# One core, Swin block then Fourier mix: the loop's tensor products in eight runs of one tile shape, joined log and root, normalisation in PSUM, eight buffers in the last stage

## The chip, the cores and the metric

One core of one Trainium2 chip runs the whole program in one launch. The time is device microseconds of that core, the median of several executions. TensorE (PE in the rows; PEld is its weight loading), VectorE (DVE), ScalarE (ACT) and GpSimd (POOL) each work through their own instructions in program order and wait for each other by semaphores; SyncE (SP) issues nearly all DMAs. A time difference of about 2% is what a comparison here calls a difference.

## The reference, cut to what matters

```python
def _L0_conv_ref(x, ...):                       # x: (8, 256, 256, 64) float32
    a = _shifted_window_attention(x, qkv_w, ...)  # windows of 4x4 tokens, 4 heads of 16
    x = x + _layernorm(a, norm1_g, norm1_b)
    h = gelu(x @ fc1_w.T + fc1_b) @ fc2_w.T + fc2_b          # 64 -> 256 -> 64
    x = x + _layernorm(h, norm2_g, norm2_b)
    return x
# inside the attention, for each window and head:
    qn = q / max(norm(q), 1e-12); kn = k / max(norm(k), 1e-12)
    attn = softmax(qn @ kn.T * scale + bias)     # 16 x 16
    out = (attn @ v) @ proj_w.T + proj_b
def _L1_conv_ref(x, w_real, w_imag):
    trend = _moving_average(x, 25)               # along axis 1, 256 long
    xf = rfft(x - trend, axis=1)[:, :128]
    ys = einsum('bmnc,cmk->bknc', xf, w_real + 1j * w_imag)
    return trend + irfft(ys padded with zeros, n=256, axis=1)
```

## The kernel before, in words

Everything is float32. The program has three stages. First a short one makes for each of the 64 channels the 256x256 matrix that stands for the whole second layer (moving average, transform, mixing, inverse) and stores it in `mix`. Then the **loop** does the first layer. Last, the **final stage** multiplies, for each of 8 images and 64 channels, the channel's matrix (`amat`) with the channel's plane (`xch`), 8 records of 256 columns on TensorE (L581), copies the product from a PSUM bank into `orow`, ScalarE the even channels (`put`, L718) and VectorE the odd ones (L912), and after each image lets ScalarE's queue store 16.8 MB (four DMAs of 4096 KB). It has `NB` = 4 buffers of `amat` and `xch` and uses 4 PSUM banks; both puts of an image wait until the image before is stored.

The loop runs over 512 groups of 512 tokens as a pipeline written out by hand: in step s every engine does a fixed list of small functions, each for the group of its stage, `i0` = s, `i1` = s-1, up to `i7` = s-7. The order of the calls at the end of each engine's `step` is the order on the engine; no scheduler moves anything. `need(engine, semaphore, group)` waits, `.then_inc(semaphore)` signals, and `there(g)` leaves a function out where its group doesn't exist. `over_groups` runs 16 steps written out, then a loop, then 7 steps that empty the pipeline.

TensorE, with the tile shape (rows x columns of the array) of each function: `turn_x` (L450, 128x128) transposes the tokens; `project_qkv` (L462, 64x128) two halves; `scores` (L479, 32x32) two parts of 64 products, each recorded as two; `weighted` (L501, 32x32) two halves; `project` (L513, 128x64); `variances` (L526 and L530, 64x64) of both layernorms; `first_layer` (L542, 64x128) and `second_layer` (L554, 128x64), two halves each. ScalarE: `keep_x` L622, `square` L629, `log_norm` L634, `root_norm` L641, `exponent` L647, `keep_o` L653, `square1` L660, `square2` L677, log and root of the two layernorms L665, L671, L682, L688, `gelu` L694 twice, and two loads of a function table (L696, L706), because Gelu and Ln/Exp lie in different tables. VectorE: `qkv_out` L805 (twice), `sum_squares` L813, `clamp` L819, `turn_k` L825, `turn_q` L831, `bias` L836, `maximum` L844, `sum_prob` L850, `invert` L857, `turn_prob` L863, `normed1` L869, `add1` L877, `normed2` L883, `gain2` L889. GpSimd: `add_o1` L944, `expand_v` L953 (two instructions), `scale_norm` L961, `norm_k` L967, `norm_q` L976, `shift` L985, `divide` L991, `add_o2` L997, `add2` L1008. SyncE loads x, 8 DMAs for a group, swaps halves of `sq1` and stores a stripe of y every four groups.

The norms of q and k go through this sequence: `square`, `sum_squares`, `clamp`, `log_norm`, `root_norm`, then `scale_norm`, `norm_k` and `norm_q` on GpSimd, then the transposes `turn_k` and `turn_q` on VectorE, then the scores:

```python
def clamp(g):                                   # VectorE, 128x64, SBUF to SBUF
    need(dve, summed, g)
    ts(ssc[ring(g, 2)], ss, 1e-24, None, ALU.max).then_inc(clamped, 1)
def log_norm(g):                                # ScalarE
    need(act, clamped, g)
```

## Time and profile before

| | before |
|---|---|
| median of three executions | 8558.72 us (lowest 8556.22) |
| profiled execution: its time | 8548.61 us |
| profiled execution: span, first to last instruction | 8546.5 us |
| TensorE busy | 8028.8 us, 94% of the span |
| VectorE, ScalarE, GpSimd busy | 5981.4, 6209.3, 5385.1 us |
| mean granted TensorE clock | 0.971 |
| chain that ended last: TensorE's share | 72% |

The loop's first transpose (L450) starts at 272.4 us and its last at 7211.5 us; the puts of the final stage start at 7313 us. Busy TensorE is an engine with something in its pipe, not one at its peak. In a timeline row the columns are the start, the time from the first start to the last end, the engine, the line, the operation, the tensors, and the count; idle time before it stands in brackets with what ended it.

### The profile page before, as it was taken

The page shows a single profiled execution, that of the slowest core. Times are in us where ns is not written, and L with a number is a line of the kernel's source. Part 1 is how long each engine was busy: PE and PEld are TensorE (multiplying, and loading weights), DVE is VectorE, ACT ScalarE, POOL GpSimd, SP SyncE. Part 2 cuts the span into 40 slices and gives each one's busy share as a digit, 9 for nine tenths or more (in the row PEclk, how much of TensorE's full clock was granted, in tenths as well). Part 3 has the DMA queues.
Part 4 walks back from the last instruction along what each step waited for, and adds up shares of the span by engine and source line. Part 5 has one row for each costly group of instructions (what it writes and reads, how often), then busy time and mean ns, then how long its engine had stood idle before and what let it go on. Part 6 is the DMA issues. An engine that isn't in the chain of part 4 may idle for free.

```text
span 8546.5 us, 659317 instructions
## 1 busy us (share of the span) xinstructions
PE 8028.8 (94%) x293684; PEld 5312.2 (62%) x293684; DVE 5981.4 (70%) x8029; ACT 6209.3 (73%) x8530; POOL 5385.1 (63%) x5127
## 2 busy tenths in 40 slices
PE   8899999999999999999999999999999999787786
PEld 5556666666666666666666666666666665566565
DVE  1468888888888888888888888888888887222221
ACT  1478888888888888888888888888888888222221
POOL 0367777777777777777777777777777777000000
PEclk9799999999999999999999999999999999898898
DMA  3122222222222222222222222222222222799999
GB/s 99 53 50 58 58 58 59 59 59 59 59 58 59 59 59 59 58 59 58 59 59 59 58 57 57 58 59 59 59 58 59 59 58 55 269 317 329 330 318 334
DMA packets 1187111, 834.30 MB, mean 98 GB/s; under 512 B 633233, under 2 KB 1043217, under 8 KB 1182867
## 3 DMA queue, kind: packets, MB, share of 16 engines
q1 hardware_dynamic: 1182404, 698.61, 31.9%
q10 hardware_dynamic: 4608, 134.22, 3.7%
q8 instruction: 80, 1.31, 0.1%
q14 instruction: 19, 0.16, 0.0%
HBM read 412.97 MB, written 285.21 MB: 82 GB/s over the span
## 4 chain that ended last, share of the span: by engine, by line
PE 72%; SPq 14%; DMA 7%; issue 4%; ACT 2%; ACTq 0%; DVE 0%; POOL 0%; POOLq 0%; DVEq 0%
PE ps L501 12%; PE ps L479 11%; PE ps L581 10%; SPq L335 10%; PE ps L554 8%; PE ps L542 8%; PE ps L462 8%; PE ps L526 5%; PE ps L513 5%; DMA out<-arena 3%; DMA arena<-in_x 3%; PE ps L450 3%; SPq L346 2%; SPq L341 2%; PE ps L424 1%
## 5 line engine op out<-in xcount | busy, mean ns | idle before, releaser
L953 POOL TENSOR_TENSOR arena<-arena 128x512 f32<-128x512 f32 x1024 | 1043.5, 1040 | 894.2 <-PE ps L501 894.2
L479 PEld LDWEIGHTS ps<-arena 32*32 32x32 f32 x131072 | 1236.4, 106 | 508.4 <-issue 502.0
L501 PEld LDWEIGHTS ps<-arena 32*32 32x32 f32 x131072 | 1289.3, 103 | 292.8 <-issue 259.1
L501 PE MATMUL ps<-arena 32*32 32x16 f32 x131072 | 1424.4, 186 | 21.1 <-issue 19.5
L479 PE MATMUL ps<-arena 32*32 32x16 f32 x131072 | 1345.1, 180 | 23.3 <-issue 16.2
L805 DVE TENSOR_TENSOR arena<-ps,arena 128x768 f32<-128x768 f32 x1024 | 980.7, 958 | 370.1 <-PE ps L462 358.0
L581 PE MATMUL ps<-xch,amat 128*128 128x256 f32 x4096 | 924.3, 389 | 285.4 <-ACT arena L718 169.5
L462 PEld LDWEIGHTS ps<-arena 64*128 64x128 f32 x8192 | 649.1, 188 | 837.4 <-issue 825.5
L985 POOL TENSOR_TENSOR arena<-arena 128x512 f32<-128x512 f32 x512 | 713.5, 1394 | 696.2 <-DVE arena L844 696.2
L694 ACT ACTIVATE arena<-ps,arena 128x1024 f32<-128x1024 f32 x1024 | 1137.4, 1111 | 7.0 <-PE ps L542 0.4
L581 PEld LDWEIGHTS ps<-xch,amat 128*128 128x128 f32 x4096 | 786.6, 195 | 423.5 <-ACT arena L718 174.7
L542 PE MATMUL ps<-arena 64*128 64x512 f32 x4096 | 1032.4, 621 | 2.8 <-ACT arena L682 2.3
L554 PE MATMUL ps<-arena 128*64 128x512 f32 x4096 | 999.9, 607 | 4.0 <-ACT arena L694 3.1
L462 PE MATMUL ps<-arena 64*128 64x192 f32 x8192 | 954.3, 352 | 5.7 <-DVE arena L805 3.2
L718 ACT ACTIVATE arena<-ps 128x512 f32 x256 | 271.0, 1066 | 935.4 <-PE ps L581 608.6
L912 DVE COPY arena<-ps 128x512 f32 x256 | 267.9, 1052 | 940.2 <-PE ps L581 625.4
L877 DVE SCALAR_TENSOR_TENSOR arena<-arena 128x512 f32<-128x512 f32 x512 | 829.9, 1621 | 23.6 <-PE ps L542 23.4
L991 POOL TENSOR_TENSOR arena<-arena 128x512 f32<-128x512 f32 x512 | 841.5, 1644 | 0.1
L665 ACT ACTIVATE arena<-ps,arena 128x512 f32<-128x512 f32 x512 | 352.0, 688 | 508.1 <-PE ps L530 505.5
L836 DVE TENSOR_TENSOR arena<-ps,arena 128x512 f32<-128x512 f32 x512 | 354.2, 692 | 515.9 <-PE ps L479 512.9
L944 POOL TENSOR_TENSOR arena<-arena 128x512 f32<-128x512 f32 x512 | 535.4, 1046 | 276.0 <-ACT arena L622 271.9
L813 DVE TENSOR_REDUCE arena<-arena 128x64 f32<-128x1024 f32 x512 | 624.9, 1220 | 106.4 <-ACT arena L629 84.0
(89 smaller groups left out, 14288.3 us busy)
## 6 DMA issues: line engine op xcount, KB each, us to landing
arena<-in_x SPq DMA_DIRECT2D x4096, 32.0 KB
arena<-arena SPq DMA_DIRECT2D x1024, 128.0 KB
y<-ystripe SPq DMA_DIRECT2D x256, 512.0 KB
amat<-mix SPq DMA_DIRECT2D x512, 256.0 KB, 3.4
xch<-y SPq DMA_DIRECT2D x512, 256.0 KB, 4.0
out<-arena ACTq DMA_DIRECT2D x32, 4096.0 KB, 27.1
mix<-amat SPq DMA_DIRECT2D x64, 256.0 KB, 2.0
wri<-in_w_real SPq DMA_DIRECT2D x64, 64.0 KB, 1.8
```

Of the source, the lines that this page charges most:

```text
L335: sp.dma_start(xin[:, p, a * C:a * C + C], src[:, p * 8:p * 8 + 8, :]).then_inc(x_in, 16)
L462: ins = mm(M[:, a, pl * 256:pl * 256 + 3 * C], xT[a * C:a * C + C, 2 * pp + pl, :], wqkv[a * C:a * C + C, :], start=True, stop=True, tile_ ...
L479: ins = mm(S(sl)[r, c0 + e:c0 + 32:2], qT[r, sl, q, e:64:2], kT[r, sl, q, e:32:2], start=True, stop=True, tile_position=(32 * cg, 32 * cg))
L501: ins = mm(PV[32 * h:32 * h + 32, b, c0:c0 + N], vexp[r, sl, h, :, :], pT[r, sl, h // 2, h % 2, :], start=True, stop=True, tile_position=( ...
L542: ins = mm(M[:, a, :], w1[a * C:a * C + C, kk * P:(kk + 1) * P], x1T[a * C:a * C + C, :], start=True, stop=True, tile_position=(a * C, 0))
L554: ins = mm(H2[a * C:a * C + C, :], w2[:, kk, :], hT[kk][:, a, :], start=(kk == 0), stop=(kk == 1), tile_position=(0, a * C))
L581: ins = mm(ps[:, j, k * T:(k + 1) * T], amat[j][:, r * T + k * P:r * T + (k + 1) * P], xch[j][:, r * T:(r + 1) * T], start=(r == 0), stop= ...
L694: f(hT[kk], M, ACT.Gelu, bias=b1[:, kk:kk + 1]).then_inc(done, 1)
L805: tt(qkv[ring(g, 4)][:, :, 4 * pp:4 * pp + 4, :].rearrange("p w s n -> p s w n"), M.rearrange("p a (s n) -> p (a s) n", s=2)[:, :, 0:3 * C ...
L877: stt(x1T, dn1, g1, xTo[ring(g, 4)], ALU.mult, ALU.add).then_inc(x1_sb, 1)
L953: tt(vexp.rearrange("p s h e d -> p (s h) e d")[:, :, e, :], qkv[ring(g, 4)][:, 2].rearrange("p s (h d) -> p (s h) d", h=HEADS), par[:, e: ...
L991: tt(pr, pr, rs.rearrange("p (n e) -> p n e", e=2).unsqueeze(2).to_broadcast([P, N, N, 2]), ALU.mult).then_inc(probs, 1)
```

## The change

TensorE's calls are put in an order in which neighbours have the same tile shape: both parts of `scores` become one run, `project` stands before `second_layer`, both halves of `project_qkv` are neighbours and get different PSUM banks (MA and MB), and `variances` comes before `first_layer`. There are 8 runs in place of 11 in a step. So that this is possible, `variances` writes to banks 4 and 5 (where scores and weighted values lie), no longer to banks 2 and 3. The logs of the two layernorms become one 128x1024 instruction, their roots another. `normed1` writes its result back to PSUM (`D1`), and `add1` reads it there; `project` therefore waits for `add1`. All lists of calls on ScalarE, VectorE and GpSimd are written in another order, with other stages for some. The final stage has `NB` = 8.

```diff
-        NB = 4
+        NB = 8
...
-        VV = MB
+        VV = ps[:, 4:6, :]
...
+        def need_norms(eng, s, g, h):
+            if there(g) or there(h):
+                eng.wait_ge(s, h.base + (h.off + 3))
...
                 def turn_x(g):
-                        after(pe, (gelu0, i6), (l1_sb, i5, i7), (xT_sb, before(g)))
+                        after(pe, (gelu1, i6), (qkvB_sb, before(g)))
                 def scores(g):
+                        if there(i5) or there(i7):
+                            need_norms(pe, l12_sb, i5, i7)
                 def project(g):
-                        need(pe, dn1_sb, before(g))
+                        need(pe, x1_sb, before(g))
                 def variances(g, h):
-                        after(pe, (xT_sb, i0), (gelu0, i6), (l1_sb, before(g), before(h)))
+                            need(pe, oT_sb, i3)
                 def first_layer(g, kk, M, done):
-                            after(pe, (l1_sb, i4, i6), (xT_sb, i0), (gelu0, before(g)))
+                            after(pe, (qkvA_sb, i0), (gelu0, before(g)))
-                            after(pe, (qkvB_sb, i0), (qkvA_sb, i0), (gelu1, before(g)))
+                            after(pe, (qkvB_sb, i0), (gelu1, before(g)))
-                scores(i2, 0)
+                scores(i2)
                 project(i4)
-                turn_x(i0)
-                scores(i2, 1)
                 second_layer(i6, 0, fc2a_ps)
                 second_layer(i6, 1, fc2b_ps)
+                weighted(i3, 0, pvA_ps)
+                turn_x(i0)
+                weighted(i3, 1, pvB_ps)
                 project_qkv(i0, 0, MA, qkvA_ps)
-                weighted(i3, 0, pvA_ps)
+                project_qkv(i0, 1, MB, qkvB_ps)
                 variances(i4, i6)
-                project_qkv(i0, 1, MA, qkvB_ps)
-                weighted(i3, 1, pvB_ps)
-                first_layer(i5, 0, MB, fc1a_ps)
-                first_layer(i5, 1, MA, fc1b_ps)
+                first_layer(i5, 0, MA, fc1a_ps)
+                first_layer(i5, 1, MB, fc1b_ps)
...
+                def log_norms(g, h):
+                    if there(g) or there(h):
+                        need_norms(act, var_ps, g, h)
+                        k = slice(0 if there(g) else 1, 2 if there(h) else 1)
+                        f(l12[:, k, :], VV[:, k, :], ACT.Ln, bias=eps).then_inc(l12_sb, 1)
+                def root_norms(g, h):
+                    if there(g) or there(h):
+                        need_norms(act, l12_sb, g, h)
+                        need(act, dn1_sb, before(g))
+                        need(act, dn2_sb, before(h))
+                        k = slice(0 if there(g) else 1, 2 if there(h) else 1)
+                        f(r12[:, k, :], l12[:, k, :], ACT.Exp, scale=-0.5).then_inc(r12_sb, 1)
...
-                act.preload_act_table_set(EXP_SET)
-                log_norm(i2)
-                square2(i7)
-                root_norm(i2)
-                exponent(i3)
-                log1(i5)
-                log2(i7)
-                root1(i5)
-                root2(i7)
-                keep_o(i4)
-                act.preload_act_table_set(GELU_SET)
-                gelu(i6, 0, MB, fc1a_ps, fc2a_ps, gelu0)
+                gelu(i6, 0, MA, fc1a_ps, fc2a_ps, gelu0)
+                gelu(i6, 1, MB, fc1b_ps, fc2b_ps, gelu1)
                 square(i1)
                 square1(i4)
-                gelu(i6, 1, MA, fc1b_ps, fc2b_ps, gelu1)
+                act.preload_act_table_set(EXP_SET)
+                log_norm(i1)
+                root_norm(i1)
                 keep_x(i0)
+                square2(i6)
+                keep_o(i3)
+                exponent(i2)
+                log_norms(i4, i6)
+                root_norms(i4, i6)
+                act.preload_act_table_set(GELU_SET)
...
-                        stt(dn1, D1, be1, r1, ALU.add, ALU.mult).then_inc(dn1_sb, 1)
+                        stt(D1, D1, be1, r12[:, 0, :], ALU.add, ALU.mult).then_inc(dn1_sb, 1)
-                        stt(x1T, dn1, g1, xTo[ring(g, 4)], ALU.mult, ALU.add).then_inc(x1_sb, 1)
+                        stt(x1T, D1, g1, xTo[ring(g, 4)], ALU.mult, ALU.add).then_inc(x1_sb, 1)
-                        stt(dn2, H2, be2, r2, ALU.add, ALU.mult).then_inc(dn2_sb, 1)
+                        stt(dn2, H2, be2, r12[:, 1, :], ALU.add, ALU.mult).then_inc(dn2_sb, 1)
```

The new lists of VectorE and GpSimd are shown below as they stand on the engines.

TensorE, one turn of the loop before (`scores`, `project`, `turn_x`, `scores`, `second_layer`, `project_qkv`, `weighted`, `variances`, `project_qkv`, `weighted`, `first_layer`):

```order
L479 MATMUL ps<-arena 32x16 x64
L228 REGISTER_ALU
L513 MATMUL ps<-arena 64x4x64 x4
L228 ISA
L228 REGISTER_ALU
L450 MATMUL ps<-arena 128x128 x4
L479 MATMUL ps<-arena 32x16 x64
L228 REGISTER_ALU
L554 MATMUL ps<-arena 64x512 x4
L228 REGISTER_ALU
L462 MATMUL ps<-arena 128x192 x4
L228 REGISTER_ALU
```

and the same turn of the changed kernel, to its end (L477 is now `scores`, L557 `second_layer`, L448 `turn_x`, L458 `project_qkv`, L529 and L533 `variances`, L545 `first_layer`):

```order
L477 MATMUL ps<-arena 32x16 x128
L228 REGISTER_ALU
L513 MATMUL ps<-arena 64x4x64 x4
L228 REGISTER_ALU x2
L557 MATMUL ps<-arena 64x512 x4
L228 REGISTER_ALU
L501 MATMUL ps<-arena 32x16 x64
L228 ISA
L448 MATMUL ps<-arena 128x128 x4
L501 MATMUL ps<-arena 32x16 x64
L228 REGISTER_ALU
L458 MATMUL ps<-arena 128x192 x8
```

The scores stand in one row of 128, and the two halves of `project_qkv` in one of 8; `variances` and `first_layer` follow them.

VectorE before, from `turn_q` to `gain2`:

```order
L831 STREAM_TRANSPOSE arena<-arena 128x1024
L869 SCALAR_TENSOR_TENSOR arena<-ps,arena 128x512
L883 SCALAR_TENSOR_TENSOR arena<-ps,arena 128x512
L857 RECIPROCAL arena<-arena 128x32
L877 SCALAR_TENSOR_TENSOR arena<-arena 128x512
L813 TENSOR_REDUCE arena<-arena 128x64
L836 TENSOR_TENSOR arena<-ps,arena 128x512
L863 STREAM_TRANSPOSE arena<-arena 128x512
L819 TENSOR_SCALAR arena<-arena 128x64
L844 TENSOR_REDUCE arena<-arena 128x32
L889 TENSOR_SCALAR arena<-arena 128x512
```

and of the changed kernel from `gain2` (L881), `sum_squares` (L805), `clamp` (L811), `turn_k` (L817), `qkv_out` twice (L797), `turn_q` (L823), `sum_prob` (L842), `invert` (L849) to `normed1` (L861) and `add1` (L869); `normed2`, `bias`, `turn_prob` and `maximum` (L836) follow and close the turn:

```order
L881 TENSOR_SCALAR arena<-arena 128x512
L805 TENSOR_REDUCE arena<-arena 128x64
L811 TENSOR_SCALAR arena<-arena 128x64
L817 STREAM_TRANSPOSE arena<-arena 128x512
L228 REGISTER_ALU
L797 TENSOR_TENSOR arena<-ps,arena 128x4x3x64 x2
L823 STREAM_TRANSPOSE arena<-arena 128x1024
L842 TENSOR_REDUCE arena<-arena 128x32
L849 RECIPROCAL arena<-arena 128x32
L861 SCALAR_TENSOR_TENSOR ps<-ps,arena 128x512
L869 SCALAR_TENSOR_TENSOR arena<-ps,arena 128x512
```

The clamp, which stood ahead of `maximum`, now stands two places behind `gain2`.

GpSimd of the changed kernel, one turn: `divide`, `add_o2`, `add_o1`, `shift`, `add2` (L1000), `scale_norm` (L953), `norm_k`, `norm_q`, `expand_v`:

```order
L983 TENSOR_TENSOR arena<-arena 128x512
L989 TENSOR_TENSOR arena<-arena 128x512
L228 REGISTER_ALU
L936 TENSOR_TENSOR arena<-arena 128x512
L977 TENSOR_TENSOR arena<-arena 128x512
L1000 TENSOR_TENSOR ystripe<-arena 128x8x16x4
L953 TENSOR_TENSOR arena<-arena 128x32
L959 TENSOR_TENSOR arena<-arena 128x512
L968 TENSOR_TENSOR arena<-arena 128x16x2x16
L945 TENSOR_TENSOR arena<-arena 128x32x16 x2
```

Before, `add2` stood behind `expand_v`; now it stands between `shift` and `scale_norm`.

## Rows read from the trace of the kernel before

**Rows 1.** Windows of L450 alone: us, engine busy (records), granted clock, DMA, GB/s

```profile
560.00:7200.00 6640.00, 323.30 (x1972) 207.51 (x1972) 1.00 0.26 58
272.00:560.00 288.00, 15.46 (x72) 9.93 (x72) 0.78 0.18 40
```

**Rows 2.** Waits of PE from 560 to 7200 us: total, times, longest

```profile
PE ps L450 <- DMA arena<-in_x: 47.0, 123, 0.6
```

**Rows 3.** Timeline of PE over one step

```profile
4013.03 1.99 PE L542 MATMUL ps<-arena 64*128 64x512 f32 x8
4014.95 1.26 PE L479 MATMUL ps<-arena 32*32 32x16 f32 x128
4016.15 1.08 PE L513 MATMUL ps<-arena 128*64 128x256 f32 x8
4017.16 0.66 PE L450 MATMUL ps<-arena 128*128 128x128 f32 x4
...
4018.94 1.94 PE L554 MATMUL ps<-arena 128*64 128x512 f32 x8
4020.81 0.92 PE L462 MATMUL ps<-arena 64*128 64x192 f32 x8
4021.66 1.42 PE L501 MATMUL ps<-arena 32*32 32x16 f32 x128
...
4026.37 1.99 PE L542 MATMUL ps<-arena 64*128 64x512 f32 x8
```

**Rows 4.** Timeline of DVE in one step

```profile
4012.84 1.23 DVE L831 STREAM_TRANSPOSE arena<-arena 128x1024 f32<-128x1024 f32 x1
...
4013.99 0.71 DVE L869 SCALAR_TENSOR_TENSOR arena<-ps,arena 128x512 f32<-128x512 f32 x1
...
4014.62 0.73 DVE L883 SCALAR_TENSOR_TENSOR arena<-ps,arena 128x512 f32<-128x512 f32 x1
...
4015.54 1.56 DVE L877 SCALAR_TENSOR_TENSOR arena<-arena 128x512 f32<-128x512 f32 x1
```

**Rows 5.** Groups by line and form, all engines: count, busy us, mean ns, idle before

```profile
L479 PE MATMUL ps<-arena 32*32 32x16 f32 x131072 | 1345.1, 180 | 23.3 <-issue 16.2 <-DVE arena L831 4.9 <-ACT arena L653 1.8
...
L694 ACT ACTIVATE arena<-ps,arena 128x1024 f32<-128x1024 f32 x1024 | 1137.4, 1111 | 7.0 <-PE ps L542 0.4
...
L805 DVE TENSOR_TENSOR arena<-ps,arena 128x768 f32<-128x768 f32 x1024 | 980.7, 958 | 370.1 <-PE ps L462 358.0
...
L836 DVE TENSOR_TENSOR arena<-ps,arena 128x512 f32<-128x512 f32 x512 | 354.2, 692 | 515.9 <-PE ps L479 512.9 <-issue 3.0
...
L985 POOL TENSOR_TENSOR arena<-arena 128x512 f32<-128x512 f32 x512 | 713.5, 1394 | 696.2 <-DVE arena L844 696.2
```

**Rows 6.** Timeline of the first groups, 283 to 286 us

```profile
283.67 0.26 ACT L634 ACTIVATE arena<-arena 128x64 f32<-128x64 f32 x1
283.96 0.35 ACT L641 ACTIVATE arena<-arena 128x64 f32<-128x64 f32 x1
...
284.39 0.24 POOL L961 TENSOR_TENSOR arena<-arena 128x32 f32<-128x32 f32 x1 [9.03 <-ACT arena L641]
284.58 1.05 POOL L967 TENSOR_TENSOR arena<-arena 128x512 f32<-128x512 f32 x1
...
285.67 0.71 DVE L825 STREAM_TRANSPOSE arena<-arena 128x512 f32<-128x512 f32 x1 [0.60 <-POOL arena L967]
```

**Rows 7.** Timeline of the last groups, 7257 to 7260 us

```profile
7257.28 1.04 POOL L997 TENSOR_TENSOR arena<-arena 128x512 f32<-128x512 f32 x1 [0.63 <-DVE arena L877]
7257.76 0.85 DVE L889 TENSOR_SCALAR arena<-arena 128x512 f32<-128x512 f32 x1
...
7258.69 1.27 POOL L1008 TENSOR_TENSOR ystripe<-arena 128x512 f32<-128x512 f32 x1 [0.36 <-DVE arena L889]
```

**Rows 8.** Windows of the final stage: us, busy PE, PEld, DVE, ACT, POOL, clock, DMA, GB/s

```profile
7425.00:7470.00 45.00, 7.91 (x28) 5.81 (x26) 0.56 (x2) 0.49 (x1) 0.00 (x0) 0.62 1.00 419
7480.00:7580.00 100.00, 100.00 (x460) 85.79 (x459) 30.02 (x29) 29.86 (x29) 0.00 (x0) 1.00 0.94 300
```

More of the change, by code:

```diff
@@ L456, in project_qkv @@
                             need(pe, xT_sb, g)
-                            after(pe, (gelu1, i6), (qkvB_sb, i1), (qkvA_sb, before(g)))
-                        else:
-                            after(pe, (qkvA_sb, i0), (gelu1, i6), (qkvB_sb, before(g)))
+                            after(pe, (gelu0, i6), (qkvA_sb, before(g)))
                         for pl in range(2):
@@ L490, in weighted @@
                             need(pe, v1_sb, g)
-                            after(pe, (biased, i2), (oT_sb, before(g)))
+                            if there(i2):
+                                need(pe, biased, i2)
+                            else:
+                                need_norms(pe, l12_sb, i5, i7)
                         else:
@@ L726, in _ @@
                 with act.Fori(0, NCH // NB) as cq:
-                    for j in (0, 2):
+                    for j in range(0, NB, 2):
                         put(b, cq, j)
@@ L889, in gain2 @@
                         ts(yg, dn2, g2, None, ALU.mult).then_inc(yg_sb, 1)
-                sum_prob(i3)
-                turn_k(i2)
-                qkv_out(i1, 1, MA, qkvB_ps, qkvB_sb)
-                turn_q(i2)
                 normed1(i5)
+                add1(i5)
                 normed2(i7)
-                invert(i3)
-                add1(i5)
-                sum_squares(i1)
                 bias(i2)
                 turn_prob(i3)
-                clamp(i1)
                 maximum(i2)
                 gain2(i7)
+                sum_squares(i1)
+                clamp(i1)
+                turn_k(i1)
                 qkv_out(i0, 0, MA, qkvA_ps, qkvA_sb)
+                qkv_out(i0, 1, MB, qkvB_ps, qkvB_sb)
+                turn_q(i1)
+                sum_prob(i2)
+                invert(i2)
             over_groups(dve, step, 4)
@@ L920, in _ @@
                 with dve.Fori(0, NCH // NB) as cq:
-                    for j in (1, 3):
+                    for j in range(1, NB, 2):
                         put(b, cq, j)
@@ L1010, in add2 @@
                            ALU.add).then_inc(y_sb, 1)
-                divide(i2)
-                add_o1(i0)
-                add_o2(i4)
-                shift(i1)
-                scale_norm(i0)
-                norm_k(i0)
-                norm_q(i0)
-                expand_v(i1)
-                add2(i6)
+                divide(i3)
+                add_o2(i5)
+                add_o1(i1)
+                shift(i2)
+                add2(i7)
+                scale_norm(i1)
+                norm_k(i1)
+                norm_q(i1)
+                expand_v(i2)
             over_groups(pool, step, 8)
```

61 lines of the change are left out of this document (20 added, 41 removed).

## The prediction

> **What bounds the kernel now.** I read the windows first, because the loop is most of the span. The loop's steps follow each other at a steady 13.47 us: 1972 records of L450 in 6640 us are 493 steps of four, at a granted clock of 1.00 [rows 1]. The reader is to see next that TensorE hardly waits there: the answer on its waits has one line, 47.0 us for the DMA of x, 0.10 us a step [rows 2]. So the step is the sum of TensorE's runs. One step without such a wait, from one first layer to the next, takes 26.37 - 13.03 = 13.34 us [rows 3]. What the other engines do costs nothing as long as each of their loops is shorter than this. The timelines of VectorE and GpSimd [rows 4, 6, 7] are read for that: not how busy they are, but how long the shortest round through them is.
>
> **TensorE, step by step.** A run pays once for its change of tile shape, and this seam can be read off two runs of one shape. `project` streams 256 columns and takes 1.01 us to the start of the next run, `second_layer` streams 512 with as many records and takes 1.87 [rows 3]. So 256 columns are 0.86, and a seam is 1.01 - 0.86 = 0.15. For the 64x128 shape: 512 columns 1.92 us, 192 columns 0.85 [rows 3], so 320 columns are 1.07, 192 are 0.64, and the seam is 0.21. A part of the scores takes 1.20 to the next run; it is busy 1.26, of which the last record's own 0.18 is the tail [rows 3, 5], so its starts fill 1.08 and the seam is about 0.11. The change takes away one seam of each: 0.15 + 0.21 + 0.11 = 0.47 us. TensorE's own sum becomes 12.87. The bounds of this are nothing, if products that stand together still drain between them, and about 0.6, if the seams of the runs that got new neighbours shrink too.
>
> The Trainium skill says two things here. "TensorEngine Tiling (Array Packing)", section Key Properties, has a change of tiling mode drain the engine; "TensorE: Matmul & The Clock Gate", Part 2, lets the drain of one matmul overlap the fill of the next. By the second alone the seam would be nothing and TensorE's step would stay at 13.34; the rows' 0.15 to 0.21 side with the first.
>
> The wait for x goes: the loads of the next group are issued when the transposes are done, as before, but the transposes stand behind `weighted`, no longer behind `project`, so the queue, which first waits for `square1` and swaps halves, has some 2 us more before x is needed. That is 0.10 us a step. Moving the swaps' consumer to the step's end leaves them about as far ahead as now; no wait for a swap shows in the loop [rows 2], and I price that at zero.
>
> **New waits of TensorE.** The scores now wait for the joined log, because the variances lie in their banks, and `project` waits for `add1`, which had another wait before. Queued behind `project` is everything else. From the end of the variances: log and root as one 128x1024 instruction each, priced by the gelu's 1.11 [rows 5], then `normed1` 0.71 [rows 4], then `add1`, with some 0.04 for each release (285.63 to 285.67 is one [rows 6]). `add1` took 1.56 with two operands in SBUF, while the two instructions that read one operand from PSUM take 0.71 and 0.73 [rows 4]. It reads PSUM now, so I take 0.71, with 1.56 as the other end. The sum is 1.11 + 1.11 + 0.71 + 0.71 + 0.16 = 3.8 us. TensorE meanwhile has `first_layer` 1.92 and the scores, 1.20 + 1.08 = 2.28: 4.2 us, so nothing is lost, by 0.4 us. At 1.56 it would lack 0.45, and the step would be 13.3. That `normed1` writes PSUM has no row; I take its 0.71 unchanged, and up to 0.4 more would be hidden.
>
> **The round through VectorE, GpSimd and ScalarE.** This decides, and it is a chain of the new lists. In a full queue an instruction of VectorE follows the one before 0.08 us before its end (13.99 - 12.84 = 1.15 for 1.23 [rows 4]). From the start of `turn_k` to that of `maximum`, all in one list: `turn_k` 0.63, `qkv_out` twice 0.88, `turn_q` 1.15, `sum_prob` 0.73 (priced as a pass of 512 elements, 0.69, plus a release, since `invert` waits for it), `invert` and `normed2` together 15.54 - 14.62 = 0.92, `normed1` 0.75 with its release, `add1` 0.63, `bias` 0.61, `turn_prob` 0.63 [rows 4 to 6]. Together 7.81 us. Then `maximum`, 0.69 + 0.04, releases GpSimd's `shift`, 1.39 [rows 5], and behind it in GpSimd's queue is `add2`, 1.27 [rows 7], ahead of `scale_norm`. From there to `turn_k` of the next group, 285.67 - 284.39 = 1.28 [rows 6]. If nothing else enters, the round is 7.81 + 0.73 + 1.39 + 1.27 + 1.28 = 12.48: under TensorE's 12.87.
>
> But `clamp` enters. VectorE issues it after `maximum`, `gain2` and `sum_squares`: 0.61, 0.3 to 0.8 and about 1.23 (1024 elements, as `turn_q` [rows 4]), that is 2.1 to 2.6 us after the start of `maximum`. GpSimd's `add2` starts at 0.73 + 1.39 = 2.1 and ends at 3.4. So the clamp falls into `add2`, though perhaps by only 0.1 us at its front. What does a TENSOR_SCALAR from SBUF to SBUF do beside a GpSimd instruction? In the loop before none meets one, but among the last groups one does: `gain2`, issued at 7257.76, lasts 0.85, until 0.29 after GpSimd's L997 ends at 7258.32 [rows 7]. It waited for GpSimd. `clamp` is the same operation on fewer elements. I take it to wait too, and to end 0.10 after `add2` (between 0.05 and that 0.29). Then `log_norm` to `turn_k` follow, 0.04 and 285.67 - 283.67 = 2.00 [rows 6]. The round is 7.81 + 0.73 + 1.39 + 1.27 + 0.10 + 0.04 + 2.00 = 13.34 us, longer than TensorE's 12.87. ScalarE has its table loaded by then, and `keep_x` behind `root_norm` comes late as well, so that TensorE spends the difference, 0.47 us, before `project_qkv`.
>
> The Trainium skill's "SBUF — State Buffer", Who interferes with whom, says that a tensor_scalar in a two-port mode and a GpSimd instruction exclude each other for a whole instruction. By that rule the clamp waits and the step is the 13.34; row and rule agree, on another size of the same operation.
>
> **Final stage.** TensorE bounds it between stores: 8 records a channel, 460 in 100 us, 1.74 us a channel, while the DMAs move 300 GB/s; during a store they move 419 and TensorE stands [rows 8]. Eight buffers let TensorE do 4 channels more ahead of the wait, 4 x 1.74 = 7.0 us, seven times. But 4 channels more (4 x 0.52 MB = 2.1 MB) are then loaded beside the store, 2.1 MB / 419 GB/s = 5.0 us that the store takes longer. The net is 2 us, seven times: 14 us. The bounds are 0 and 49.
>
> **The sum.** Loop: 493 x (13.47 - 13.34) = 64 us. Final stage 14. The first and last groups stay. 8548.6 - 64 - 14 = 8471 for a profiled execution, and the median of the runs shown is 10 us above it: about **8480 us**. The round's terms are good for 0.2 us a step either way, 100 us, and its own range is 8385 to 8600.
>
> **Rivals.** First, the clamp doesn't wait for GpSimd, because it is small or slips in ahead of `add2`. Then TensorE's 12.87 bounds: 493 x 0.60 = 296 us, 8549 - 296 - 14 + 10 = 8249, and as low as 8190 with the larger seams. For it: no row shows a clamp waiting, and the margin at the front is 0.1 us. Against it: the row of `gain2`, and the two lists, which are timed by each other, so that the meeting recurs in every step. Second, the change doesn't do what it says: joined products drain as before, TensorE's step stays at 13.34 without the wait for x. That gives the forecast's own time by another way. Third, the slower side: the clock. Now it is 1.00 throughout the loop, but between 272 and 560 us, where the engines still wait for each other, it is granted at 0.78, and there 72 records are 18 steps in 288 us, 16.0 us each [rows 1]. The change brings 0.47 us of idle TensorE into each step, and puts both runs of `weighted` around the transposes. If that keeps the loop in the state of its first 288 us, it costs 493 x 2.53 = 1250 us, 9730 us. It decides from 0.35 us a step on, a seventh of that, which a mean clock of 0.97 in the loop would show. Against it: the wait at each step's x did not lower the clock.
>
> **How the numbers follow.** The forecast 0.58; the first rival 0.22; joined products that drain as before 0.06; the clock, or a chain longer than I count, 0.14, of which 0.12 beyond 2%. What a measurement of this kernel can tell is 2%, 171 us: below 8388 or above 8730. Faster is the first rival and 0.08 of the forecast, 0.30; slower 0.12; within 2% 0.58. The range reaches over the first rival: 8200 to 8600.
>
> **What the profile would show.** Right: TensorE's runs of 2.3 us (scores), 2.7 (project and second layer) and 1.5 (both qkv halves); clamps with a mean near 1.2 us in place of 0.15, each ending with an `add2`; `add1` at 0.71; `turn_k` waiting for `norm_k`, and TensorE waiting before `project_qkv` for ScalarE; about 13.3 us a step. Wrong: clamps of 0.15 beside a busy GpSimd, and TensorE without waits at 12.9 us. The prediction fails too if ScalarE's joined instructions take far over 1.11, for then the scores and `project` wait for them.

## The result and the profile after

| | before | changed |
|---|---|---|
| median | 8558.41 us (4 runs, 8556.22 to 12912.76) | 8644.44 us (4 runs, 8639.17 to 8647.62) |
| profiled execution: time, span | 8548.61, 8546.5 us | 8647.62, 8645.4 us |
| mean granted TensorE clock | 0.971 | 0.944 |
| first to last L450, now L448 | 272.4 to 7211.6 us | 273.1 to 7353.9 us |
| first put of the final stage | 7313.2 us | 7464.3 us |

The changed kernel takes 1.0101 of the time before, with a 95% interval of 1.0084 to 1.0119. It is 1% slower. One of the four runs of before, 12912.76 us, was in a slow state and does not enter the ratio; the other three lie between 8556.22 and 8558.72 us. The forecast was 8480 us within 8200 to 8600, and 8644 lies above that range. By the marks of the table the loop lost 7080.8 - 6939.2 = 141.6 us and the stretch behind it 8.8, while the final stage from its first put on gained (8546.5 - 7313.2) - (8645.4 - 7464.3) = 52.2. With the 0.7 us by which the loop starts later the sum is 99 us of span, in the two profiled executions (the medians are 86 apart).

Windows of L448, the columns those of [rows 1]:

```profile
272.00:560.00 288.00, 12.72 (x60) 8.10 (x60) 0.71 0.14 31
560.00:7200.00 6640.00, 305.33 (x1940) 204.38 (x1940) 0.97 0.26 57
```

1940 records are 485 steps of 13.69 us where [rows 1] had 493 of 13.47, and the clock, 1.00 before, is 0.97. Waits of all engines in the same stretch:

```profile
DVE arena L817 <- POOL arena L959: 999.6, 485, 2.6
POOL arena L983 <- DVE arena L849: 835.5, 456, 3.9
...
ACT arena L636 <- DVE arena L811: 464.5, 484, 1.6
...
POOL arena L953 <- ACT arena L643: 403.6, 482, 1.4
...
PE ps L458 <- ACT arena L624: 104.6, 350, 0.5
```

ScalarE's `log_norm` (L636) waits for `clamp` (L811), GpSimd's `scale_norm` (L953) for ScalarE, VectorE's `turn_k` (L817) for GpSimd, and `project_qkv` (L458) for `keep_x` (L624): the round of the prediction, link by link. And the chain that ended last, on the page of the profile, has changed hands; TensorE had 72% of it before:

```profile
POOL 36%; issue 29%; PE 18%; DVE 9%; DMA 4%; ACT 2%; POOLq 0%; SPq 0%; ACTq 0%; DVEq 0%
```

The clamp itself, all 485 of the stretch (min, median and max ns), and the timeline around one:

```profile
L811 DVE TENSOR_SCALAR arena<-arena x485: 1126/1204/1224, 565.3 to 7189.3; 128x64 f32<-128x64 f32 x162
```

```profile
4008.32 1.27 POOL L1000 TENSOR_TENSOR ystripe<-arena 128x512 f32<-128x512 f32 x1
4008.44 1.21 DVE L811 TENSOR_SCALAR arena<-arena 128x64 f32<-128x64 f32 x1
...
4009.69 0.26 ACT L636 ACTIVATE arena<-arena 128x64 f32<-128x64 f32 x1 [0.84 <-DVE arena L811]
4009.97 0.35 ACT L643 ACTIVATE arena<-arena 128x64 f32<-128x64 f32 x1
4010.23 0.58 ACT L624 ACTIVATE arena<-ps 128x512 f32<-128x512 f32 x1
...
4010.86 1.57 PE L458 MATMUL ps<-arena 64*128 64x192 f32 x16
```

GpSimd's `add2` (L1000) starts 0.12 us before the clamp and ends at 4009.59; the clamp ends at 4009.65, 0.06 after it.

The second thing to see is on TensorE. A timeline of PE, with the two runs of `weighted` (L501) around `turn_x` (L448), and `project_qkv` (L458) behind them:

```profile
4020.54 1.40 PE L501 MATMUL ps<-arena 32*32 32x16 f32 x128
4021.90 0.63 PE L448 MATMUL ps<-arena 128*128 128x128 f32 x4
4022.46 1.26 PE L501 MATMUL ps<-arena 32*32 32x16 f32 x128
4024.00 2.93 PE L458 MATMUL ps<-arena 64*128 64x192 f32 x16 [0.28 <-ACT arena L624]
```

`project_qkv` takes 2.93 us where it took 1.57 one step earlier. Windows of the two steps, all engines (busy PE, PEld, DVE, ACT, POOL, then clock, DMA, GB/s), show why: the granted clock is 1.00 in one and 0.89 in the other.

```profile
4000.00:4013.00 13.00, 12.80 (x568) 8.60 (x564) 10.87 (x16) 11.06 (x14) 10.02 (x11) 1.00 0.18 40
4013.38:4026.86 13.48, 13.07 (x560) 9.43 (x556) 10.97 (x15) 11.06 (x14) 10.49 (x12) 0.89 0.18 40
```

The trace's clock records have 117 such falls from 2.4 to 1.2 GHz between 605 and 6945 us, and none there in the kernel before. Each begins within 0.6 us of the end of the second run of `weighted`; the one above begins at 4023.78 us. Falls are counted so below for every kernel (605 to 6945 us is steady loop in all of them; the 130, 189 and 34 in some expectations are counts from 560 to 7200 us).

The third is the run of the joined scores (L477). Most take 2.29 to 2.4 us, as predicted; in every fourth step, the one whose queue also stores y, it takes 2.7 to 3.4 us, with small gaps spread over it and no wait at its head:

```profile
4043.21 3.26 PE L477 MATMUL ps<-arena 32*32 32x16 f32 x256
4046.39 1.08 PE L513 MATMUL ps<-arena 128*64 128x256 f32 x8
```

From a scores' start to the next run it is 2.55 us in the mean of 66 steps between 3000 and 3900 us. The runs over 2.7 us, 113 of 464 between 605 and 6945 us, are called the long scores below.

### The profile page after: what moved, and what is told of

It is laid out like the page before. It is cut to its first block, busy times and chain, and to the rows that moved or that the text cites. A ratio compares the mean times of both kernels' runs of the same rounds, so it can differ in the third digit from the quotient of the medians.

```text
span 8645.4 us, 657801 instructions
## 1 busy us (share of the span) xinstructions
PE 8039.8 (93%) x293684; PEld 5581.6 (65%) x293684; DVE 6023.9 (70%) x8029; ACT 6003.5 (69%) x7510; POOL 5196.4 (60%) x5127
## 4 chain that ended last, share of the span: by engine, by line
POOL 36%; issue 29%; PE 18%; DVE 9%; DMA 4%; ACT 2%; POOLq 0%; SPq 0%; ACTq 0%; DVEq 0%
PE ps L583 9%; POOL arena L945 8%; POOL ystripe L1000 6%; POOL arena L936 5%; POOL arena L983 5%; POOL arena L977 5%; POOL arena L968 4%; DMA out<-arena 3%; PE ps L458 3%; POOL arena L959 2%; DVE ps L861 1%; PE ps L422 1%; DVE arena L823 1%; DVE arena L797 1%; PE ps L529 1%
## 5 line engine op out<-in xcount | busy, mean ns | idle before, releaser
L501 PEld LDWEIGHTS ps<-arena 32*32 32x32 f32 x131072 | 1255.9, 103 | 556.0 <-issue 543.2
L477 PEld LDWEIGHTS ps<-arena 32*32 32x32 f32 x131072 | 1238.5, 105 | 539.6 <-issue 502.9
L477 PE MATMUL ps<-arena 32*32 32x16 f32 x131072 | 1315.4, 180 | 98.7 <-issue 45.6
L501 PE MATMUL ps<-arena 32*32 32x16 f32 x131072 | 1373.0, 186 | 34.3 <-issue 32.2
L983 POOL TENSOR_TENSOR arena<-arena 128x512 f32<-128x512 f32 x512 | 626.0, 1223 | 949.7 <-DVE arena L849 898.9
L674 ACT ACTIVATE arena<-ps,arena 128x1024 f32<-128x1024 f32 (+1 forms) x514 | 571.3, 1111 | 788.7 <-PE ps L533 782.4
L458 PE MATMUL ps<-arena 64*128 64x192 f32 x8192 | 991.6, 392 | 117.9 <-ACT arena L624 111.8
L817 DVE STREAM_TRANSPOSE arena<-arena 128x512 f32<-128x512 f32 x512 | 364.7, 712 | 1056.7 <-POOL arena L959 1056.7
L688 ACT ACTIVATE arena<-ps,arena 128x1024 f32<-128x1024 f32 x1024 | 1086.0, 1111 | 6.1
L945 POOL TENSOR_TENSOR arena<-arena 128x512 f32<-128x512 f32 x1024 | 1043.4, 1040 | 39.2 <-PE ps L501 39.2
L545 PE MATMUL ps<-arena 64*128 64x512 f32 x4096 | 1024.5, 618 | 0.0
L797 DVE TENSOR_TENSOR arena<-ps,arena 128x768 f32<-128x768 f32 x1024 | 931.7, 938 | 129.1 <-PE ps L458 129.1
L557 PE MATMUL ps<-arena 128*64 128x512 f32 x4096 | 1001.3, 602 | 4.8 <-ACT arena L688 4.8
L458 PEld LDWEIGHTS ps<-arena 64*128 64x128 f32 x8192 | 811.1, 224 | 169.1 <-ACT arena L624 156.8
L977 POOL TENSOR_TENSOR arena<-arena 128x512 f32<-128x512 f32 x512 | 713.2, 1393 | 324.5 <-DVE arena L836 324.5
L710 ACT ACTIVATE arena<-ps 128x512 f32 x256 | 272.4, 1086 | 879.4 <-PE ps L583 548.1
L545 PEld LDWEIGHTS ps<-arena 64*128 64x128 f32 x4096 | 352.5, 186 | 673.8 <-issue 496.1
L936 POOL TENSOR_TENSOR arena<-arena 128x512 f32<-128x512 f32 x512 | 538.9, 1052 | 272.6 <-ACT arena L624 272.6
```

Source lines behind the costliest of these rows:

```text
L458: ins = mm(M[:, a, pl * 256:pl * 256 + 3 * C], xT[a * C:a * C + C, 2 * pp + pl, :], wqkv[a * C:a * C + C, :], start=True, stop=True, tile_ ...
L477: ins = mm(S(sl)[r, c0 + e:c0 + 32:2], qT[r, sl, q, e:64:2], kT[r, sl, q, e:32:2], start=True, stop=True, tile_position=(32 * cg, 32 * cg))
L501: ins = mm(PV[32 * h:32 * h + 32, b, c0:c0 + N], vexp[r, sl, h, :, :], pT[r, sl, h // 2, h % 2, :], start=True, stop=True, tile_position=( ...
L545: ins = mm(M[:, a, :], w1[a * C:a * C + C, kk * P:(kk + 1) * P], x1T[a * C:a * C + C, :], start=True, stop=True, tile_position=(a * C, 0))
L557: ins = mm(H2[a * C:a * C + C, :], w2[:, kk, :], hT[kk][:, a, :], start=(kk == 0), stop=(kk == 1), tile_position=(0, a * C))
L688: f(hT[kk], M, ACT.Gelu, bias=b1[:, kk:kk + 1]).then_inc(done, 1)
```

## The experiments

After the result I had three theories. **Lock**: the clamp, held by `add2`, makes the round, and the rest is small. **Clock**: the falls cost the loop more than the lock, and would be there without it. **Load**: the scores' long runs, beside the load of x, are what the joined product pays. Times of "before" in the ratios are 8550 to 8560 us, run beside each kernel.

**1. The clamp as a reduction.** The maximum with 1e-24 is taken over pairs, the sum and a stored constant. `sum_squares` writes its sums beside the constants; nothing else changes.

```diff
-ts(ssc[ring(g, 2)], ss, 1e-24, None, ALU.max).then_inc(clamped, 1)
+# ss is 2 wide: [:, :, 0] the sums, [:, :, 1] set once to 1e-24
+dve.tensor_reduce(ssc[ring(g, 2)], ss, AX.X, ALU.max).then_inc(clamped, 1)
```

> The changed kernel, with the clamp made by a TENSOR_REDUCE (maximum of the sum and a stored 1e-24, the same values) in place of the TENSOR_SCALAR. Theory A (the clamp waits for GpSimd's add2, and the order of TensorE's runs lowers the clock): the clamp falls from 1.20 to about 0.2 us, TensorE's wait before project_qkv goes, undisturbed steps take 12.8 to 12.9 us, but the granted clock in the loop stays near 0.97, because weighted, turn_x and weighted still stand together; mean step 13.2 to 13.4, time 8400 to 8500. Theory B (TensorE's idle time before project_qkv, which the clamp makes, lowers the clock): the falls go too, clock 1.00, step about 13.0, time about 8320. Theory C (the clamp is on no path, TensorE's own joined runs are slow): no change, 8640.

Measured: 8511.55 us (5 runs), 0.9958 of before [0.9944, 0.9972], 133 us under the changed kernel. The clamp now takes 0.29 us (473 of them), beside the same busy GpSimd:

```profile
L814 DVE TENSOR_REDUCE arena<-arena x473: 285/287/290, 564.7 to 6893.4; 128x64 f32<-128x128 f32 x158
```

TensorE has no wait for data left in the loop, and an undisturbed step is 12.75 to 12.80 us (12.80 in the mean of the 277 steps with neither a fall nor long scores). The loop spans 6943.0 us, 137.8 less than with the lock. But there are still 121 falls, again each within 0.6 us of the end of the second `weighted`, and the mean step is 13.40. So the lock is real and costs 0.27 us a step; the falls and the long scores stay without it.

**2. The clamp out of `add2`'s way.** The instruction is the old one; GpSimd's `add2` stands behind `expand_v` instead.

> The changed kernel, clamp as it is, but GpSimd's add2 moved behind expand_v, so that GpSimd is idle when the clamp is issued. If it is the GpSimd instruction beside it that holds the clamp: clamp about 0.15 us and the same time as the kernel with the reduced clamp, within 0.5%. If the clamp is slow by itself or by its place on VectorE: still 1.2 us, 8640 or more.

Measured: 8503.48 us (4 runs), 0.9944 [0.9928, 0.9961]; 121 falls.

```profile
L811 DVE TENSOR_SCALAR arena<-arena x473: 195/195/198, 569.8 to 6896.7; 128x64 f32<-128x64 f32 x158
```

The same TENSOR_SCALAR takes 195 ns when no GpSimd instruction runs beside it, and the time is that of experiment 1 within 8 us. It is the meeting that costs, not the operation by itself.

**3. The lock in the kernel before.** Its `clamp` is issued behind `maximum` and `gain2`, where GpSimd runs `shift` (1.40 us); all else is as before.

> The kernel before, with the clamp issued behind maximum and gain2, where GpSimd runs shift (1.4 us). If a GpSimd instruction holds the clamp: clamp 0.9 to 1.3 us instead of 0.15 in this kernel too, and the log waits for it. TensorE is the bound there and the log's users have slack, so the time moves by less than 0.5%. If the clamp's slowness belongs to the changed kernel alone: 0.15 us.

Measured: 8687.19 us (a single execution; 13 of before, run beside it, lie between 8555 and 8564), 1.5% over before. My expectation that the time moves by less than 0.5% was wrong.

```profile
L819 DVE TENSOR_SCALAR arena<-arena x484: 1203/1214/1223, 559.2 to 7198.8; 128x64 f32<-128x64 f32 x162
```

```profile
ACT arena L634 <- DVE arena L819: 696.6, 481, 1.6
...
PE ps L526 <- ACT arena L677: 255.7, 483, 0.7
```

Moving one instruction of 153 ns in VectorE's list costs the old kernel 129 us: the clamps are held for 1.21 us, ScalarE starts its log 1.45 us late each step, and TensorE waits 0.53 us before the variances. The clock had no fall here, in spite of that wait in each of 483 steps; this kernel has the order of products of the kernel before, which has none either.

**4 and 5. The final stage's buffers alone.** The changed kernel with NB = 4, and the kernel before with NB = 8.

> The changed kernel with NB 4 in the last stage. By the two traces (146.8 against 153.6 us for an image) it gives back about 52 us: 8696. By the prediction's term, 14 us: 8658.

> The kernel before with NB 8 alone. By the traces 8558 - 52 = 8506; by the prediction's term 8544. The loop stays at 13.47 us a step.

Measured: 8708.21 us (1.0182 [1.0165, 1.0199]) and 8496.70 us (0.9936 [0.9919, 0.9953]; before was 8552.56 beside both). Eight buffers are worth 64 us in the changed kernel and 56 in the old one. The images of the final stage, by ScalarE's first put of each after a store, follow each other every 147.0 us in the changed kernel and every 154.5 us in the one before, and the wait for the stores, 331.4 us over seven stores, is with NB = 4 the same, 328.3.

**6. The first normalisation in PSUM, alone, in the kernel before.**

```diff
-stt(dn1, D1, be1, r1, ALU.add, ALU.mult).then_inc(dn1_sb, 1)
+stt(D1, D1, be1, r1, ALU.add, ALU.mult).then_inc(dn1_sb, 1)
-stt(x1T, dn1, g1, xTo[ring(g, 4)], ALU.mult, ALU.add).then_inc(x1_sb, 1)
+stt(x1T, D1, g1, xTo[ring(g, 4)], ALU.mult, ALU.add).then_inc(x1_sb, 1)
```

with `project` waiting for `x1_sb` in place of `dn1_sb`.

> The kernel before with its first normalisation kept in PSUM (normed1 and add1 write D1, and project waits for add1), all else as it was. By my price add1 falls from 1.6 to 0.7 us on VectorE and no run of TensorE changes: 13.47 us a step, 8558 us within 0.3%. If less work on VectorE also lowers TensorE's waits there, it can be the 0.1 us of the x wait at most, 8510 us. If project comes to wait for add1, it is slower, 0.1 to 0.3 us a step, 8600 to 8700 us.

Measured: 8574.55 us (10 runs), 1.002 [1.001, 1.0029]. Groups of DVE between 560 and 6900 us:

```profile
L869 DVE SCALAR_TENSOR_TENSOR ps<-ps,arena 128x512 f32<-128x512 f32 x470 | 338.9, 721 | 0.0
...
L877 DVE SCALAR_TENSOR_TENSOR arena<-ps,arena 128x512 f32<-128x512 f32 x469 | 312.3, 666 | 0.1
```

`add1` is 0.67 us instead of the 1.56 of [rows 4], `normed1` writes PSUM at 0.72, and nothing is gained, for 0.9 us a step comes off an engine that bounds nothing; the kernel is 17 us slower, and why was not looked for.

**7 to 9. The transposes and the store moved, with the reduced clamp.** First `turn_x` ahead of both runs of `weighted`; then, instead, the store of y issued ahead of the queue's swaps; then both.

> The kernel with the reduced clamp, and on TensorE turn_x ahead of both halves of weighted (which then are neighbours: one seam less, about 0.1 us). In the traces every fall of the clock in the loop follows weighted, turn_x, weighted. Theory A (that stretch of small products lowers the clock): without it the falls go, the granted clock is 1.00, the mean step loses 0.36 + 0.1 us, 8511 - 230 = about 8280. Theory B (any idle time or the 32-row products as such do it, wherever turn_x stands): falls as before, 130 or so, step -0.1, about 8460. It could also lose: both halves of weighted together are 2.5 us of small products.

> The kernel with the reduced clamp, and on SyncE the store of y ahead of the swap, so that it no longer stands between the swap and the next load of x. Every fourth step the scores take 3.3 us and not 2.3, and there the load of x, held up behind the store, runs beside them. Theory A (the load of x beside 32x32 products slows them): the scores' slow runs go, step -0.2 us, 8511 - 100 = 8410. Theory B (the store's own traffic or the loop's branch does it): the slow runs stay, 8511, or more, because the store now runs beside the scores.

> Both edits. If both theories A hold and add up: step 12.8 us or less, about 8180 to 8230. If only one holds, the time of that one.

Measured: 8658.46 (1.0116 [1.0099, 1.0133]), 8520.75 (0.9955 [0.9941, 0.997]) and 8654.89 us (1.0113 [1.0096, 1.013]). With `turn_x` in front there are 91 falls, and a new wait, of the second run of `weighted` for the first, which now ends right ahead of it:

```profile
PE ps L501 <- PE ps L501: 108.3, 462, 0.4
```

The two halves take 3.17 us together where the pair took about 2.6, so the order was no test of the clock alone. The falls stand where they stood, around the end of the second `weighted` (90 of the 91 from 0.95 us ahead of it to 1.07 behind), so `weighted` need not stand on both sides of the transposes for them. With the store first, the scores shrink, from at most 3.29 to 2.92 us and from 2.59 to 2.49 in the mean (3000 to 3900 us), as expected of Load; but the falls rise from 121 to 176, and the time stays. With both it is 119 falls. These three told that the number of falls depends on the order, of the products and of the DMA queue, and that more falls can take back what another edit gives; they did not tell what sets them.

**10 and 11. The stretch broken up.** With the reduced clamp, one half of the second layer stands between the first run of `weighted` and the transposes; then the same with the early store.

```diff
 scores(i2)
 project(i4)
 second_layer(i6, 0, fc2a_ps)
-second_layer(i6, 1, fc2b_ps)
 weighted(i3, 0, pvA_ps)
+second_layer(i6, 1, fc2b_ps)
 turn_x(i0)
 weighted(i3, 1, pvB_ps)
```

> The changed kernel with the clamp as a reduction (as before), and with the first-half second layer moved ahead of the first weighted product, the other half between it and the transposes: weighted and turn_x and weighted no longer stand in one stretch, at the price of one more seam. Theory A, the clock falls because the two runs of 32x32 products stand around the transposes: the falls (130 in the loop of the kernel with the reduced clamp) go, the clock is 1.00, the step is 12.78 (undisturbed) + 0.2 for the seam + 0.2 for the slow scores = 13.15 us, and the time 8390 to 8410 us. Theory B, the falls come from the joined scores or from small products in any order: over 100 falls stay, the loop's mean clock stays near 0.97, and the time is 8540 to 8600 us.

> As the kernel with the split order, with the store of y issued ahead of the swaps, so that the load of x is not held up behind it while the scores run. If the order has ended the falls, the scores' slow runs of 3.3 us shrink to at most 2.9 and the time is 30 to 60 us under that of the split order alone. If falls stay, there are more of them than without the store moved (189 against 130 in the earlier pair), and the time is the same within 20 us or longer.

Measured: **8350.78 us** (4 runs, 0.976 [0.9744, 0.9777]) and **8294.60 us** (4 runs, 0.969 [0.9674, 0.9706]). Windows of L448 from 560 to 6900 us, of the reduced clamp (experiment 1), the split, and the split with the early store, in that order:

```profile
560.00:6900.00 6340.00, 297.91 (x1892) 199.18 (x1892) 0.97 0.26 59
```

```profile
560.00:6900.00 6340.00, 318.11 (x1936) 203.61 (x1936) 0.99 0.27 60
```

```profile
560.00:6900.00 6340.00, 320.28 (x1948) 204.76 (x1948) 0.99 0.27 61
```

473, 484 and 487 steps; 121, 33 and 27 falls. Theory A of the expectation held in kind, and the time came out better than it said, because the extra seam cost nothing net. Not one of the falls that are left stands at `weighted` or the transposes. All 33 and all 27 begin between 0.2 us ahead of the end of a run of long scores and 0.6 behind it, as this one at 3018.19 us in the last kernel, where `project` takes 1.61 us instead of 1.08 and half a second layer 1.98 instead of 1.06:

```profile
3014.90 2.92 PE L477 MATMUL ps<-arena 32*32 32x16 f32 x256
3017.78 1.61 PE L513 MATMUL ps<-arena 128*64 128x256 f32 x8
3019.11 1.98 PE L557 MATMUL ps<-arena 128*64 128x512 f32 x4
```

So the split ended one kind of fall, and another took its place, a quarter as often. The length of the scores alone does not make it: the changed kernel has runs of up to 3.4 us and no fall behind any. An undisturbed step of the last kernel:

```profile
4016.40 2.50 PE L477 MATMUL ps<-arena 32*32 32x16 f32 x256
4018.86 1.08 PE L513 MATMUL ps<-arena 128*64 128x256 f32 x8
4019.75 1.06 PE L557 MATMUL ps<-arena 128*64 128x512 f32 x4
4020.74 1.26 PE L501 MATMUL ps<-arena 32*32 32x16 f32 x128
4021.93 1.08 PE L557 MATMUL ps<-arena 128*64 128x512 f32 x4
4022.94 0.66 PE L448 MATMUL ps<-arena 128*128 128x128 f32 x4
4023.53 1.26 PE L501 MATMUL ps<-arena 32*32 32x16 f32 x128
4024.75 1.57 PE L458 MATMUL ps<-arena 64*128 64x192 f32 x16
```

The second layer in two runs is 0.99 + 1.01 us where one run was 1.84; but `weighted` followed by it takes 1.19, where followed by the transposes it took 1.37. And the early store now pays (56 us), where with many falls it did not.

**12 and 13. What stands between.** Both start from the last kernel. One has the whole second layer between `weighted` and `turn_x`; the other has `turn_x` ahead of the first `weighted`, and the whole second layer between the two runs.

> The kernel with the split order and the early store, with both halves of the second layer between the first weighted product and the transposes (project, weighted, second layer whole, turn_x, weighted): as many changes of tile shape, and 1.0 us more of dense 128-row products between the two runs of 32x32 products. Theory A, the remaining falls (34) come from the 32x32 runs that stand near the transposes: no more than 10 falls, the step goes from 13.3 to 12.9 or 13.0 us in the mean, 8240 to 8270 us. Theory C, they come from the slow scores (2.9 us, every fourth step) or from the number of 32x32 runs in a step: 30 to 40 falls and 8290 to 8300 us. A wait of the first weighted product, which now comes 1 us earlier, would give it back.

> As the last, with the transposes behind project and ahead of the first weighted product (project, turn_x, weighted, second layer whole, weighted): the transposes now touch one run of 32x32 products and the other is 3.2 us away. By theory A no falls and 8240 to 8270 us. By theory C falls as many as with the split order (34). The transposes come 3 us earlier, so a wait for x or for the second gelu can show: 0.1 us a step, 8290 to 8320 us.

Measured: 8595.57 (1.0049 [1.0033, 1.0066]) and 8495.49 us (0.9936 [0.992, 0.9953]), both misses of the 8240 to 8270; the second is also beyond the 8290 to 8320 that its expectation gave for a wait. Each has a new wait, of the first from 560 to 6900 us, then of the second:

```profile
PE ps L501 <- DVE arena L858: 211.9, 436, 0.5
```

```profile
PE ps L448 <- ACT arena L688: 196.6, 408, 0.5
```

In the first, `weighted` comes 1 us earlier and meets the wait for `turn_prob` (L858), and the falls stay: 30, as theory C said (they come from the slow scores), each of them behind long scores of 2.93 us or more. In the second, the transposes wait for the second gelu; but there is no fall at all in 472 steps. Its scores are shorter too, 2.79 us at the most.

**14. No wait, and the transposes ahead.** `project`, half a second layer, `turn_x`, `weighted`, half, `weighted`.

> The kernel with the split order and the early store, with the transposes between the first half of the second layer and the first weighted product (project, half, turn_x, weighted, half, weighted). In the order with the transposes right behind project the clock fell 2 times only, but TensorE waited 0.5 us a step there for the second gelu; half a second layer ahead of it, 1.0 us, should cover that wait. Theory A (what lowers the clock is a run of 32x32 products on both sides of the transposes, or close ahead of them): few falls, no wait, 12.80 us a step and 12.9 in the mean, 8230 to 8260 us. Theory D (the wait itself kept the clock up in the last kernel, and any order without waits has its falls): 30 or more falls, 8290 us or more.

Measured: **8296.48 us** (4 runs, 0.9693 [0.9677, 0.9709]), 36 us above the upper end of what theory A said. Windows of L448:

```profile
560.00:6900.00 6340.00, 321.13 (x1952) 205.56 (x1952) 1.00 0.27 61
```

488 steps of 12.99 us, 8 falls against 27 with the transposes behind `weighted`, and no wait for data in the loop. The fewer falls bring nothing here, because the second run of `weighted` takes 1.38 us in this order and 1.23 in the other. So an order without a wait can have few falls (theory D, which said 30 or more, is out). That it is the place of the transposes is not shown: the 8 falls again stand at the end of long scores, 2.93 to 2.97 us, and this order has fewer and shorter ones, 103 with a mean of 2.84 against 121 with 2.91. Whether the order acts on the clock by itself or through the scores, and whether the wait kept the last falls away in experiment 13, was not tried.

## Why the prediction was wrong, point by point

**TensorE's seams** were sized rightly. The prediction took off 0.47 us a step, to 12.87; undisturbed steps without the lock are 12.75 to 12.80, inside its bound of 0.6. That joined products still drain is refuted: the scores' run is 2.29 to 2.4 us, `project` with the whole second layer 0.89 + 1.85.

**The x wait** went, as said, and the two **new waits of TensorE** priced at nothing cost next to nothing: log and root took 1.11 and 1.06, `normed1` 0.67 into PSUM and `add1` 0.75, and `project` waited for `add1` 10.3 us in 49 of 485 steps.

**The round with the clamp in it** was right, mechanism and nearly size. The clamp takes 1.20 us and ends 0.06 after `add2` (predicted 0.10). The round, from one `turn_k` to the next where the clock stays up, is 13.14 us, predicted 13.34; half of the difference lies in VectorE's list, in the step at 4000 us 7.70 from `turn_k` to `maximum` and not 7.81. Removing the lock brought 137.8 us of loop (experiment 1), 0.27 a step. The first rival, that the clamp slips by, did not happen; its 8249 us would not have come even then, for a reason below.

The Trainium skill's "SBUF — State Buffer", Who interferes with whom, has a tensor_scalar in a two-port mode and a GpSimd instruction block each other for a whole instruction, and a tensor_reduce never, on trn2. Experiments 1 to 3 agree, with 153 to 195 ns alone, 1204 to 1214 beside a GpSimd tensor_tensor, and 287 for a reduction that isn't held.

**The step that failed is that TensorE's clock stays at 1.00**, which every term of the sum took for granted. The third rival had the clock, its signature (0.97 in the loop, as came), and one of its two causes. It was dismissed with "the wait at each step's x did not lower the clock". That sentence rests on less than it says, for [rows 2] has 123 such waits in 493 steps, not one at each step; and it is beside the point, because waits of such a size do not lower the clock by themselves. A kernel with 0.53 us of wait in each step has no fall (experiment 3), one with no wait has 121 (experiment 1), and one with 0.42 has none (experiment 13). What the prediction named in passing, both runs of `weighted` around the transposes, is what the experiments bear out for this kernel: its 117 falls all begin at the end of that stretch, and between experiment 1 and the split one call is moved and all 121 there go, while 33 come at the long scores. The clock also fell behind a joined `weighted` with the transposes ahead of it (experiment 7), so the arrangement is one of several that do it, and what they have in common is open. The price was wrong too: it is not the 2.53 us a step of the first 288 us. `project_qkv` takes 2.93 - 1.57 = 1.36 us more in a fall, and the step 14.24 - 13.11 = 1.13, by the table below; with the long scores' share this is what took the forecast's gain away.

**The joined scores** are the second term that failed, and cost about as much as the falls. They were priced at the sum of their parts less a seam, 2.28. Every fourth run takes longer, 3.05 in the mean, and the mean of all is 2.55 in the changed kernel, some 0.2 us over the undisturbed run; the step with a long one takes 1.23 us more, and the 0.5 that its scores do not explain was not traced. That a part of 1.2 us did not pay it in the kernel before (1.24 and 1.23 in the mean there) I can only note. The load of x behind the store of y is the likely neighbour, since an earlier store shrank the long runs in experiments 8 and 11; but the store itself moved with it, and what slows TensorE was not separated.

The steps of the changed kernel between 605 and 6945 us, from one `turn_x` to the next, sorted by what happens in them:

| | steps | mean, us |
|---|---|---|
| neither | 281 | 13.11 |
| a fall of the clock | 70 | 14.24 |
| long scores | 65 | 14.34 |
| both | 47 | 15.07 |
| all | 463 | 13.66 |

So the round sets 13.11, and falls and long scores add 0.54 a step between them, 0.17 by the falls alone, 0.17 by the long scores alone and 0.20 by the steps with both. Against 13.47 before, this is the loss of the loop: at 13.11 throughout, an estimate from this table, it would have been faster than before by more than was forecast. The forecast's round was 0.2 too long, which made its miss smaller; that is luck.

**The final stage** was forecast at 14 us within 0 to 49, and gave 52 in the profiled runs and 56 to 64 alone. The 49 us for four channels ahead of each store were about right; the term that failed is the 5.0 us by which the added loads should lengthen each store. The wait for the stores grew by 3 us over all seven, not by 35.

**The sum** took the first and last groups as unchanged, and that failed too. Of the 141.6 us the steady loop accounts for some 496 x 0.22 = 109; the other 33 were lost at its start, where 60 records of L448 now stand in the 288 us that held 72 [rows 1], at a clock of 0.71 instead of 0.78. What sets the clock there was not tried. The result is within 2% of before, the class that had 0.58, but 44 us above the end of the range: the clock was weighed as all (1250 us) or nothing, and no case stood between. A slower scores run was weighed nowhere.

## What to carry to other kernels

When an edit reorders TensorE's runs, check the granted clock of the loop before anything else: the profile here had TensorE 93% busy, and much of the loss was in a clock of 0.97, not in a wait. Look at what stands right ahead of each fall. Here it was a stretch of 32x32 products: `weighted` with the transposes, or the long scores. A dense product moved into the first took 1.9% off this kernel (8511.55 to 8350.78), and its seam cost nothing net. A VectorE instruction of 0.15 us from SBUF to SBUF can be the start of the round that sets the step: look what GpSimd does at its moment, in the order in which it will stand, and write it as a reduction if they meet, or move one of the two. And repair the parts in combination: the changed order with the lock removed, one call moved and an early store is 8295 us, 3.1% under before, though the order as it was written is 1% slower.

## What the runs showed of the hardware that was not expected

- The clock falls without TensorE being idle. In the loop of the kernel with the reduced clamp no wait for data shows, and the clock falls 121 times in 6340 us; 0 to 176 times in the others, by the order of the products and of the DMA queue. Nearly all falls begin near the end of a run of 32x32 products: the second `weighted` in the changed kernel and in experiments 1, 2 and 7 to 9 (there 24 of the 176 of experiment 8 at the scores), the long scores in experiments 10 to 12 and 14.
- A seam depends on the pair. A run of 32x32 products followed by 128x64 ones takes 1.19 us to the next start, by 128x128 transposes 1.37, by 64x128 products 1.23 to 1.38.
- A run of 256 small products is slowed from 2.3 to as much as 3.4 us in steps where a load of x runs behind a store; its two halves apart took 1.24 and 1.23 us in the mean. Which traffic slows it is not shown.
- A run that waits for the run right ahead of it on TensorE (experiment 7, the second `weighted` for the first) pays for it: 108.3 us in 462 waits, 0.23 each and 0.4 at the most; with the transposes between the two (experiment 1) no such wait shows.
